# Clearing ring tiles on VectorE, and six more chunks of rows fetched by ScalarE, in a relational graph layer

## The reference

```python
h = relu(layernorm(x))                       # 12500 x 256
hx = einsum('ni,rio->rno', h, weight)        # 8 relations
agg = segment_sum(hx[edge_type, src], dst)   # over 212500 edges
out = x + agg * 0.5**0.5 + h_bias + (h @ loop_weight) * 0.5**0.5
```

## Time and profile before

| | |
|---|---|
| median of three executions | 2043.67 us |
| the profiled execution | 2044.47 us |
| its span, first to last instruction | 2042.7 us |
| TensorE matmul busy | 1529.7 us, 75% |
| VectorE busy | 1335.0 us, 65% |
| ScalarE busy (issuing of DMAs not counted) | 342.8 us, 17% |
| GpSimd busy | 1522.1 us, 75% |
| DMA engines, mean share busy | four to five tenths in the main loop |

### The profile page before, as it was taken

How to read it: one execution, slowest core, us unless ns; L and a number is a source line. 1 busy time by engine, 2 the same in 40 slices (tenths; PEclk the granted TensorE clock), 3 DMA queues, 4 the chain that set the end, 5 groups by cost and what they waited for, 6 DMA issues and landing times.

```text
span 2042.7 us, 45665 instructions
## 1 busy us (share of the span) xinstructions
PE 1529.7 (75%) x10568; PEld 1179.3 (58%) x10568; DVE 1335.0 (65%) x4141; ACT 342.8 (17%) x427; POOL 1522.1 (75%) x1610
## 2 busy tenths in 40 slices
PE   0027788788887887888877878878778878878878
PEld 0015566566666665666666656656666666656656
DVE  7856666666766666666666666666666666666662
ACT  5640111111111111111110210210210210210110
POOL 7777777777777777777777777777777777777773
PEclk9997888888888889888989889888888889888888
DMA  9964444444444444444444444444444444444442
GB/s 357 340 226 122 125 134 134 125 133 134 126 133 131 129 134 128 131 134 127 131 134 127 133 133 126 134 133 125 134 134 126 133 133 127 134 130 129 134 129 70
DMA packets 141489, 290.71 MB, mean 142 GB/s; under 512 B 38542, under 2 KB 86026, under 8 KB 138142
## 3 DMA queue, kind: packets, MB, share of 16 engines
q0 software_dynamic: 76896, 210.08, 35.8%
q10 hardware_dynamic: 49922, 54.25, 8.1%
q1 hardware_dynamic: 14396, 23.45, 3.7%
HBM read 262.02 MB, written 25.60 MB: 141 GB/s over the span
## 4 chain that ended last, share of the span: by engine, by line
POOL 38%; PE 24%; DMA 22%; issue 13%; DVE 1%; ACT 1%; POOLq 0%; SPq 0%; ACTq 0%; DVEq 0%
POOL rows L400 38%; DMA rows<-h_table,src_i 18%; PE psum L921 16%; PE psum L991 7%; DMA h_table<-room 4%; PE psum L914 1%; ACT psum L466 1%; DMA room<-x 1%; PE psum L926 0%; DVE stats L602 0%; PE psum L890 0%; PE psum L973 0%; DVE mv L609 0%; PE psum L905 0%; POOLq L85 0%
## 5 line engine op out<-in xcount | busy, mean ns | idle before, releaser
L400 POOL DMA_INDIRECT rows<-h_table,src_i x1506 | 1428.1, 948 | 461.7 <-issue 423.3
L787 DVE TENSOR_TENSOR room<-room,psum 128x256 f32 x1661 | 696.5, 419 | 582.0 <-PE psum L991 493.8
L921 PE MATMUL psum<-w_sb,room 128*128 128x256 f32 x3072 | 1001.6, 444 | 0.0
L991 PE MATMUL psum<-onehot,rows 128*128 128x128 f16 x6260 | 674.4, 238 | 388.7 <-DMA rows<-h_table,src_i 384.4
L991 PEld LDWEIGHTS psum<-onehot,rows 128*128 128x128 f16 x6260 | 480.0, 106 | 682.5 <-DMA rows<-h_table,src_i 509.8
L921 PEld LDWEIGHTS psum<-w_sb,room 128*128 128x128 f32 x3072 | 591.2, 219 | 49.1
L726 DVE TENSOR_SCALAR onehot<-lane,base_i 128x128 f16<-128x128 f16 x1565 | 434.0, 278 | 64.1
L489 ACT COPY room<-zeros 128x2048 f32<-128x2048 f32 x94 | 178.5, 1899 | 1459.9 <-DVE result L754 1212.6
L926 PE MATMUL psum<-w_sb,own_hT 128*128 128x256 f32 x384 | 119.7, 394 | 0.0
L389 POOL DMA_INDIRECT raw<-x,src_i x96 | 93.0, 969 | 31.1 <-issue 28.9
L1035 PE MATMUL psum<-unfit_p,ones 128*1 128x4 f32 x2 | 0.2, 166 | 114.4 <-DVE room L644 114.4
(11 more groups left out here) (57 smaller groups left out, 276.1 us busy)
## 6 DMA issues: line engine op xcount, KB each, us to landing
rows<-h_table SPq DMA_DIRECT2D x4608, 1.0 KB
rows<-h_table ACTq DMA_DIRECT2D x2944, 1.0 KB
rows<-h_table,src_i POOLq DMA_INDIRECT x1506
own<-h_table ACTq DMA_DIRECT2D x97, 128.0 KB
own_x<-x ACTq DMA_DIRECT2D x97, 128.0 KB
out<-result ACTq DMA_DIRECT2D x97, 128.0 KB
room<-x SPq DMA_DIRECT2D x12, 1024.0 KB, 7.9
h_table<-room ACTq DMA_DIRECT2D x12, 1024.0 KB, 8.5
```

Of the source, the lines that this page charges most:

```text
L400: nc.gpsimd.indirect_dma_start(out=rows[:, q % NB, :], out_offset=None, in_=table[:, :], in_offset=bass.IndirectOffsetOnAxis(ap=src_i[:, c ...
L787: nc.vector.tensor_tensor(window, window, sum_of(c).rearrange("p (a w) -> p a w", w=W), ALU.add).then_inc(added, 1)
L921: nc.tensor.matmul(ps_out[:, 0:D], nodes[:, m, :], w_sb[:, h, r, :], start=(m == 0), stop=False)
L991: last = nc.tensor.matmul(sum_of(c)[:, h * P:(h + 1) * P], now[:, part * D + h * P:part * D + (h + 1) * P], onehot[:, k, :], start=(part = ...
```

## The change

ScalarE's `clear_tile` is removed from its loop, and VectorE clears the slot of tile s - 3 with a memset right after `scale_product` in step s, up to tile 93. `fetch_rows` handles 40 rows an iteration over the chunks' common row number, in blocks of at most 32 rows and within a chunk; it stands ahead of `scale_raw` and is called in every iteration until the 29 chunks are done. ScalarE's chunks are chunk 4 of the steps 7, 10, 13, 16, 19, 23, 26, ... 96 (five in 16 steps). SyncE gets one chunk more, the last but one of all (chunk 10 of the last step). The lists of row offsets, made by VectorE and TensorE ahead of the loop, come from nine ranges instead of four.

```diff
-    SCALAR_STEPS = range(7, STEPS - 1, 4)
-    SCALAR_ROWS = [(0, 32), (32, 64), (64, 96), (96, 128)]
+    SCALAR_STEPS = [range(7, STEPS - 1, 16), range(10, STEPS - 1, 16), range(13, STEPS - 1, 16), range(16, STEPS - 1, 16), range(19, STEPS - 1, 16)]
+    SCALAR_ROWS, SCALAR_TILES = 40, 1
...
-    sync_chunks = [K * s + SYNC_K for s in sync_steps]
+    sync_chunks = [K * s + SYNC_K for s in sync_steps] + [E_CHUNKS - 2]
...
-            def clear_tile(t):
-                act.wait_ge(out_ready, t + 1)
-                nc.scalar.copy(ring[:, :, ring_slot(t):ring_slot(t) + P],
-                               zeros[:, :].unsqueeze(1).broadcast_to([P, HR, P])).then_inc(cleared, 1)
...
             def fetch_rows(t):
...
+                first = t * SCALAR_ROWS // SCALAR_TILES
+                end = min((t + 1) * SCALAR_ROWS // SCALAR_TILES, P * len(scalar_chunks))
+                while first < end:
+                    j, a = first // P, first % P
+                    b = min(P, a + end - first, a + SYNC_LOAD)
+                    if a == 0 and j >= AB:
+                        act.wait_ge(summed, scalar_chunks[j - AB] + 1)
...
+                    for p in range(a, b):
+                        act.dma_start(rows[p:p + 1, NB + SB + j % AB, :].bitcast(mybir.dt.uint8),
+                                      table_bytes[:, bass.ds(start[p - a], ROW_BYTES)]
+                                      ).then_inc(scalar_landed[j % AB], 16)
+                    first += b - a
...
                     if t >= 1:
                         store_tile(t - 1)
-                        if t <= TILES - RING + 1:
-                            clear_tile(t - 1)
                     copy_hT(t)
                     own_tile(t + 2)
                     own_x_tile(t + 1)
+                    fetch_rows(t)
                     if raw_step(t + 2) is not None:
                         scale_raw(raw_step(t + 2))
-                    if t < len(SCALAR_ROWS) * len(scalar_chunks):
-                        fetch_rows(t)
...
+            def clear_tile(t):
+                nc.vector.memset(ring[:, :, ring_slot(t):ring_slot(t) + P], 0.0).then_inc(cleared, 1)
...
                     if k == 1 and s > 2:
                         scale_product(s - 3, P, (s - 3) % 2, ps_out)
+                        if s - 3 <= TILES - RING:
+                            clear_tile(s - 3)
```

More of the change, by code:

```diff
@@ L76, in relational_graph_layer @@
     sync_steps = sorted(s for steps in SYNC_STEPS for s in steps)
-    sync_chunks = [K * s + SYNC_K for s in sync_steps]
+    sync_chunks = [K * s + SYNC_K for s in sync_steps] + [E_CHUNKS - 2]
     list_ranges = [(K * steps[0] + SYNC_K, K * steps.step, len(steps)) for steps in SYNC_STEPS]
-    scalar_chunks = [K * s + SCALAR_K for s in SCALAR_STEPS]
-    list_ranges.append((K * SCALAR_STEPS[0] + SCALAR_K, K * SCALAR_STEPS.step, len(SCALAR_STEPS)))
+    scalar_steps = sorted(s for steps in SCALAR_STEPS for s in steps)
+    scalar_chunks = [K * s + SCALAR_K for s in scalar_steps]
+    list_ranges += [(K * steps[0] + SCALAR_K, K * steps.step, len(steps)) for steps in SCALAR_STEPS]
+    list_ranges.append((E_CHUNKS - 2, 1, 1))
     listed = [a + d * i for a, d, n in list_ranges for i in range(n)]
@@ L509, in fetch_rows @@
             def fetch_rows(t):
[L510 to L520, removed]
+                first = t * SCALAR_ROWS // SCALAR_TILES
[5 more added lines that the diff above has]
+                        act.wait_ge(summed, scalar_chunks[j - AB] + 1)
+                    q = listed.index(scalar_chunks[j])
+                    _, start = nc.values_load_multi_w_load_instructions(
+                        row_offsets[q:q + 1, a:b], engines=[mybir.EngineType.Activation],
+                        min_val=0, max_val=(N - 1) * ROW_BYTES,
+                        skip_runtime_bounds_check_because="the sources of edges are nodes")
+                    for p in range(a, b):
[3 more added lines that the diff above has]
+                    first += b - a
             def copy_hT(t, to=own_hT):
```

## The result

The changed kernel takes 2110.16 us (median, 2108.46 to 2111.34) beside 2042.18 us (2040.67 to 2045.21) of the kernel before on the same chip: a ratio of 1.0331, 95% interval 1.0315 to 1.0348. It is 3.3% slower; 2036.1 had been forecast, and the upper end of the range was 2041.5. The span went from 2042.7 to 2106.7 us, and TensorE's mean granted clock from 0.878 to 0.912, so the clock isn't the cause.

A forecast was written before the change was run, and what follows sets the result against it. The prediction took GpSimd's gathers, 1.255 us each, to bound the kernel. Six fewer that count save 7.5 us, everything else nothing: span 2042.7 to 2036.9, less 0.8 for the runs' median, 2036.1 us; range 2033.5 to 2041.5.

The forecast's parts named there:

- What bounds the kernel, and the gathers: GpSimd's gathers set the pace at 1.255 us each; 1506 become 1499.
- the six gathers' 7.5 us: Of seven gathers taken off GpSimd, the six in steps up to 96 shorten what ends last: 7.5 us.
- The memset: VectorE's 94 clears of 128x2048 f32 take 2.1 us each, 197 us in all, and fit in its idle time.
- The lock between them: Rival: VectorE's memset holds up the first gather starting in it, mean 1.5 us, 94 times; about 2177 us; chance 4%.
- Forty rows an iteration: ScalarE's loop: a normal iteration takes 16.6 us; eight with one normalisation take 139 us against 154 us, so it fits.
- The part ahead of the rows: ScalarE's iteration before its first row: shrinks from 3.8 to about 2.9 us without the clear.
- The rows, 13.3 us: ScalarE's 40 row fetches in an iteration, at 0.33 us each: 13.3 us.
- The raw step: A step in which ScalarE also normalises raw rows, one in eight: 5.8 us more.
- ScalarE's queue becomes the pacer: Rival: ScalarE's rows slow from 0.33 towards 0.389 us, its iterations outlasting the steps from 0.38; 2055 us; chance 4%.
- the lead of one step: ScalarE's chunks are complete one step early, so 19 us came off the 30 us loss of a slow ScalarE queue.
- Raw steps cost nothing: In 11 steps ScalarE's square root comes 5.7 to 8.6 us later; VectorE's stall is absorbed before GpSimd, costing nothing.
- SyncE's chunk: SyncE's 37th chunk, in the last step: 50 us more of rows, ending near 2003 less 7.5 us, delaying nothing else.

The follow-up runs named there:

- light SyncE: The kernel before with 19 chunks for SyncE instead of 36, GpSimd gathering the rest: 2062.08 us, 1.0093; 2593.6 us, 0.8531 on a slow chip.

## Why the prediction was wrong

**What bounds the kernel, and the gathers: right.** 1499 gathers of 947 ns came, and 17 moved gathers cost 19 of the 21 us that they were priced at. The bound was GpSimd's pace, and the six gathers' 7.5 us were there to be had as long as nobody got later.

**The memset: right.** It takes 1.765 us, at the lower bound of 1.77 that the slope of two small memsets gave; I had taken 2.1, from the larger of them. It begins inside one gather and covers the start of the next, and neither that one nor the one behind it is moved. GpSimd, then VectorE, changed kernel; it answers to the earlier trace rows:

```profile
1015.30 0.95 POOL L402 DMA_INDIRECT rows<-h_table,src_i  x1 [0.30 <-issue]
1016.56 0.95 POOL L402 DMA_INDIRECT rows<-h_table,src_i  x1 [0.31 <-issue]
1017.81 0.95 POOL L402 DMA_INDIRECT rows<-h_table,src_i  x1 [0.30 <-issue]
...
1015.67 1.76 DVE L750 MEMSET room<- 128x2048 f32 x1 [0.38 <-PE psum L996]
```

The lock between them, 4%, is out: the pitch stays at 1.25 us. The short memset that I had held against it was misread: it runs from 1023.03 to 1023.30, and the gather of 1022.19 ends at 1023.14, so the memset lay only partly inside it.

**Forty rows an iteration: the step that failed.** Eight iterations were to take 139 us against 154 us of eight steps. They take 160 (8 x 19.96). Three terms of that sum were too small:
- The part ahead of the rows, 2.9 us without the clear. Its median is 3.74 us; it is 3.81 in the kernel with 32 rows and no clear, and was 3.77 before with it. The clear had run beside the register loads (L515), which take 2.2 us of the queue; taking it away freed nothing there. The second block's loads make one pitch of 1.46 us out of one of 0.34, 1.1 us more and not 0.4. Together about 1.5 us an iteration.
- The rows, 13.3 us. From first to last row the median is 15.05 us with the second block; less the block's 1.1 us that is 13.9, some 0.6 over. Part of it was there from the start, as the 32 rows that I priced from, 10.61 us, are fast ones: their median before is 10.80 us, which makes 13.5 for 40. The rest, 0.4 us, came with the load.
- The raw step, 5.8 us over a normal one. It is 9.9, because beside the normalisation the next store waits 3.7 us for VectorE's result, which is itself late from VectorE's stall.

8 x (1.5 + 0.6) + 4.1 is 21 us, and 139 + 21 is 160.

**The rival that came.** It is "ScalarE's queue becomes the pacer", which I gave 4%: reached at 0.38 us a row, it said, and the table has 0.381 (second loads included). I had argued against it with one iteration, where ScalarE's rows ran at 0.33 beside SyncE's. But that was the queue with 385 us of idle time in a loop where the DMA engine kept up. Its price, 2055, was too low by the same three terms: 5.9 us over eight steps makes 67 us over the 91 iterations, and the lead of one step that I took off is not seen in the result. That its condition was met at 0.381 is partly luck: the second block's loads and the slow raw step, which it didn't have, did as much as the price of a row.

**Raw steps cost nothing: wrong by its input, right in its mechanism.** The kernel with 32 rows shows a cushion that absorbs 4.7 us. The stall became 10.4 us, where VectorE was to wait 3 to 8. Between the load of x and the first row I had put 1.2 us. It had been 2.38 us before the change, from the end of this line of the kernel before to the first row at 1016.33, and is 2.34 at raw step 44:

```profile
1013.50 0.45 ACTq L502 DMA_DIRECT2D own_x<-x  x1
```

The rows ahead of the root take up to 17 us and not 13.3. And the cushion got thinner: TensorE sums a chunk only when the last sixteenth of it has landed, 10 us after the gather's start and not 4. GpSimd runs 11 gathers ahead, 13.8 us, and a landing at 13 us uses that up.

**SyncE's chunk: not what ended last.** Its last rows take 0.405 us and end at 2053.56, in place of 0.389 and 2003 less 7.5. They are not in the chain:

```profile
2000.09 53.47 SPq L328 DMA_DIRECT2D rows<-h_table  x132
```

**What is shown and what isn't.** Shown: undoing the order gives back 10 of 68 us where GpSimd sets the pace; memset and order are free with 32 rows and a light SyncE; ScalarE's queue has next to no slack with forty rows, in either order; the last of 16 parts of a gather lands 6 us later, and it follows the single rows.

Not settled by a run: whether the queue is too full by its own length or by the DMA engine that slows its rows. The first iterations give an estimate. While the last part still lands within 3.9 to 7.1 us (from 243 to 299 us), an iteration takes 18.35 us with nothing idle in it, in both orders. With the order changed, seven of these and one of 28.3 (10 us over, as a raw step) are 157 us against the 154 us of eight steps: too full already, by about 3 of the 6 us. With the order back a raw step is 4.7 us over a normal one, and the eight make 152 us, which would fit; there it is the slower rows that fill the queue. By this estimate both are at work in the change, and the prediction had neither.

Not run on a chip that takes 2043 us: forty rows with a light SyncE, 32 rows with 36 chunks of SyncE and the change's other parts, and the memset alone. On a chip that takes 2043 us no kernel tried here beats the kernel before. On the others the kernels with the light SyncE take 12 to 15% less than it, and none of the rest beats it by more than half a per cent.

## What to carry to other kernels

A queue that issues many small transfers has to be summed up like an engine, with its register loads, its waits and what used to run beside it: when work is moved away from it, look at which of it lay on the queue's own path. Price a transfer at the load that the change will make, not at the load of the row it is read from, and look at the last part of a landing, since a mean DMA share can stay at 0.46 while one of sixteen engines falls behind. A stall that an experiment removes only counts for what comes back: here 112 us of waits went away and 10 us came back. And find out what sets the pace on the chip in hand before a result is carried over: moving 17 chunks from SyncE to GpSimd cost 19 us on one chip and saved 453 us on another.

## What the runs showed of the hardware

- The last of a gather's 16 parts takes 2.94 us (median) with 5376 single 1 KB rows on two other queues in a run, 4.04 with 7552 and 10.11 with 8448, while the 15th stays at 2.7 to 2.8 us.
- A 1 KB row issued alone makes one 1 KB packet and one of 4 bytes; SyncE's rows go one at a time (1 of 3794 packets overlaps the one ahead of it), with a median of 46 ns a packet.
- A memset of 128x2048 f32 on VectorE takes 1.765 us, 0.86 ns a column. The page "VectorE: DVE Perf Modes" of the Trainium skill, section "Zero memsets can be issued as uint32 (trn2)", has one cycle per element, at 0.96 GHz 2.13 us as an estimate; the measurement decides.
- Chips differ: the kernel before takes 2043 us on some and 2997 to 3046 (medians) on others, with a row of SyncE's at 0.61 us and not 0.389, TensorE's mean granted clock at 0.78 and not 0.88, and gathers at nearly the same 947 to 950 ns. The runs don't say why.
- A contiguous row of 1 KB described as four pieces left the number of packets unchanged.
